# Half passes in the row halves of TensorE's array for the queries' projection, with other first stages, router products, last stages and order

## The reference

```python
# layer 0, attention: 32 heads, low rank (192) for queries, 64 for keys and values
q = rms_norm(x @ q_a_w, q_a_ln_w) @ q_b_w          # 192 = 128 + 64 rows of the product
ckv = x @ kv_a_w                                    # 64 latent, 64 rotary columns
scores = q_pass @ k_pass.T + rope(q_rot) @ rope(k_rot).T
out = softmax(causal(scores)) @ v @ o_w
# layer 0: graph attention on the context (top-k mask), then 7 experts, top 2, and a shared one
gate = x @ Wr + br                                  # 8 columns: the router
# layer 1: attention with 16 heads, bilinear attention on the context, feed-forward of 1024
h = silu(x @ w_gate.T) * (x @ w_up.T);  y = h @ w_down.T
```

## Time and profile before

| | |
|---|---|
| median of 3 runs | 673.74 us (673.16 to 674.34) |
| the profiled execution, its own time | 674.2 us |
| its span, first to last instruction | 672.3 us |
| PE busy | 651.7 us (97%), 5342 matmuls |
| DVE, ACT, POOL busy | 524.2, 502.5, 389.5 us |
| granted clock of TensorE | 0.997 |

### The profile page before, as it was taken

The page is one execution under the profiler, slowest core; times in us unless marked ns, Lnnn a source line. Parts: engine busy times, 40 slices in busy tenths (PEclk is TensorE's granted clock), DMA queues, the critical chain, the costliest instruction groups (busy, mean ns, idle before and its releaser), DMA issues.

```text
span 672.3 us, 15731 instructions
## 1 busy us (share of the span) xinstructions
PE 651.7 (97%) x5342; PEld 557.9 (83%) x5342; DVE 524.2 (78%) x1684; ACT 502.5 (75%) x1305; POOL 389.5 (58%) x646
## 2 busy tenths in 40 slices
PE   8899999999999999999999999999989999999996
PEld 5589988989888899889877888889878887778885
DVE  2799988996999799767889945557798878858455
ACT  4799778878688885898887866665658786876544
POOL 3388658457664845698769455545872321445543
PEclk9999999999999999999999999999999999999998
DMA  8763022214213211310032012111020000011201
GB/s 259 188 186 86 18 71 59 77 26 118 49 56 103 49 50 47 95 33 2 1 96 63 1 54 87 48 49 47 1 95 5 3 3 4 3 48 48 94 1 63
DMA packets 35048, 40.17 MB, mean 60 GB/s; under 512 B 7052, under 2 KB 27798, under 8 KB 34968
## 3 DMA queue, kind: packets, MB, share of 16 engines
q1 hardware_dynamic: 34424, 38.84, 19.8%
q10 hardware_dynamic: 544, 0.33, 0.2%
HBM read 29.05 MB, written 1.05 MB: 45 GB/s over the span
## 4 chain that ended last, share of the span: by engine, by line
PE 82%; DVE 7%; ACT 4%; SPq 2%; issue 2%; DMA 1%; POOL 1%; DVEq 0%; POOLq 0%; ACTq 0%
PE bank L1242 72%; PE bank L1256 8%; SPq L2762 1%; PE bank L1542 1%; ACT probs L1922 1%; DMA xT_plain<-in_xT 1%; POOL qT L2487 1%; DVE bn L2034 1%; DMA qT<-xT_plain 1%; DVE ctx_pair_lo L2011 1%; DVE y L2011 1%; DVE probs L2162 1%; DVE g_pair_lo L2011 0%; ACT x L1684 0%; ACT xT_hi L1677 0%
## 5 line engine op out<-in xcount | busy, mean ns | idle before, releaser
L2484 POOL TENSOR_SCALAR probs<-probs,soft 128x256 f32<-128x256 f32 (+1 forms) x256 | 104.9, 432 | 52.1 <-DVE soft L2170 51.0
L1784 ACT ACTIVATE probs<-probs,soft 128x256 f32<-128x256 f32 (+1 forms) x256 | 113.2, 448 | 12.0 <-DVE soft L2162 11.1
L2487 POOL TENSOR_TENSOR w_split_lo<-w_raw,w_split_hi 128x512 fp32r<-128x512 f32 (+2 forms) x57 | 74.3, 1311 | 67.9 <-ACT w_split_hi L1677 67.7
L1242 PE MATMUL bank<-xT_hi,w_split_hi 128*128 128x512 f32 x256 | 103.8, 405 | 3.7 <-DVE xT_lo L2014 2.5
L1242 PE MATMUL bank<-xT_lo,w_split_hi 128*128 128x512 f32 x256 | 100.5, 393 | 0.0
L1242 PE MATMUL bank<-keyT,qT 128*64 128x192 f32 (+3 forms) x1024 | 80.4, 302 | 1.3 <-POOL qT L2487 1.3
L1242 PEld LDWEIGHTS bank<-keyT,qT 128*64 128x64 f32 x1024 | 74.2, 137 | 8.9 <-issue 3.6
L1242 PE MATMUL bank<-xT_hi,w_split_lo 128*128 128x512 f32 x192 | 75.5, 393 | 0.0
L2487 POOL TENSOR_TENSOR qT<-qT,xT_plain 64x512 f32<-64x512 f32 x44 | 56.5, 1283 | 31.8 <-DMA qT<-xT_plain 29.7
L2162 DVE CUSTOM_DVE_ANT_0 probs<-bank,mask 128x128 f32<-128x128 f32 (+1 forms) x192 | 58.0, 330 | 17.2 <-PE bank L1242 16.2
L1677 ACT ACTIVATE probsT<-bank 128x384 f32<-128x384 f32 x128 | 53.6, 494 | 13.9 <-PE bank L1256 13.4
(11 more groups left out here) (259 smaller groups left out, 1820.6 us busy)
## 6 DMA issues: line engine op xcount, KB each, us to landing
qT<-xT_plain SPq DMA_DIRECT2D x88, 64.0 KB, 2.0
w_raw_heads<-in_w_o SPq DMA_DIRECT2D x8, 512.0 KB, 4.6
w_raw<-in_w_nopeT SPq DMA_DIRECT2D x8, 384.0 KB, 3.1
qT<-rope_buf SPq DMA_DIRECT2D x40, 64.0 KB, 2.0
w_raw<-in_w_gateT SPq DMA_DIRECT2D x8, 256.0 KB, 2.7
w_raw<-in_w_upT SPq DMA_DIRECT2D x8, 256.0 KB, 3.1
w_raw<-in_w_downT SPq DMA_DIRECT2D x8, 256.0 KB, 3.6
w_raw<-in_L_ffn_Wup SPq DMA_DIRECT2D x7, 256.0 KB, 2.6
```

Of the source, the lines that this page charges most:

```text
L1242: return t.matmul(out, lhsT, rhs, start=start, stop=stop, skip_group_check=shared)
L1784: ins = s.activation(p[:, at], p[:, at], ACT.Exp, bias=st[:, 0, r:r + 1], scale=-1.0, accum_out=st[:, 1, r:r + 1])
L2484: return g_.tensor_scalar(out, in0, s1, s2, op0, op1)
L2487: return g_.tensor_tensor(out, in0, in1, op)
```

## The change

1. `q` is cut in two steps. `q_full` makes the four whole-array matmuls of each bank. `q` makes the fifth of each bank over 64 rows alone: the rotary weights' hi rows now stand in rows 64 to 127 and the latent ones' in rows 0 to 63 (`rest_rows`), so the two matmuls lie in different row halves. The memset of `qaT.lo` goes.
2. The start: `down_T` loses the keys' transposes to a step `key_T`; DVE's `key_scale` is a step apart from `down_scale`; a Sqrt on ACT at the start loads its table early; the first q's wait for less (`TURNED_FOR`); `adj_w`, `adj_qk`, `adj_sim 0` and both `down` steps come earlier; the second load of tokens goes ahead of the first weights; the first `qT` buffer lies in other memory.
3. The router: the tokens are loaded and the router's weights, split in hi and lo (16 columns), stream; `route_gate` and ACT's copy go.
4. `out1` puts its two bias matmuls together.
5. The end: `f_end` is cut in `f_mid` (hidden tiles 4 to 6) and `f_end` (tile 7), in the order `f_mid 0, f_mid 2, f_end 0, f_mid 1, f_end 1`; the last store is issued by ACT.
6. PE's order and the due times are new throughout, and so are the planner's costs.

```diff
-down 0, w_k 0, down 1, w_q 0, down_T 0, w_v 1, w_k 1, q 0 0 0, down_T 1, w_q 1, adj_w, w_v 0, adj_qk, q 0 0 1,
-q 1 0 0, s 0 0 0, s 1 0 0, q 1 0 1, adj_sim 0, s 0 0 1, s 1 0 1, q 1 1 0, pT 0 0 0, q 1 1 1, pT 0 0 1, pT 1 0 0,
+down 0, down 1, w_k 0, adj_w, w_q 0, adj_qk, w_v 0, down_T 0, key_T 0, adj_sim 0, w_v 1, q_full 0 0 0, q 0 0 0,
+w_k 1, down_T 1, q_full 0 0 1, key_T 1, w_q 1, q 0 0 1, q_full 1 0 0, q 1 0 0, w_k 2, s 0 0 0, q_full 1 1 0, q 1 1 0,
...
+EVERY_TURNED = [(name, h) for h in range(NHALF) for name in ("down_T", "key_T")]
+TURNED_FOR = {("q", 0, 0, 0): [("down_T", 0)], ("q", 0, 0, 1): [("down_T", 0), ("key_T", 0)]}
+MID_TILES = [[(0, j) for j in range(TB)], *[[(1, j)] for j in range(TB)]]
+LAST_STORED = (B - 1, TB - 1)
...
+    def rest_rows(kind, low=False):
+        return slice(QREST, P) if (kind == 1) != low else slice(0, QREST)
...
                 for kind in (1, 0):
                     out = wait_bank(("q", n, g, p, ("lat", "rot")[kind]))[:, :]
                     first, rest = (w_q[:, c, kind, 2 * p:2 * p + 2, :] for c in range(2))
-                    mm3(out, first, qaT[:, 0, at], True, False)
-                    mm(out, rest.hi, qaT.hi[:, 1, at], False, False)
-                    mm(out, rest.hi, qaT.lo[:, 1, at], False, True).then_inc(q_ready.sem, 1)
+                    mm3(out, first, qaT[:, 0, at], True, False, True)
+                    mm(out, rest.hi, qaT.hi[:, 1, at], False, False, True)
+            elif name == "q":
+                n, g, p = k
+                rest, at = group_q(g).hi[:, 1, :, 2 * p:2 * p + 2, :], slice(n * HALF, (n + 1) * HALF)
+                for kind in (1, 0):
+                    rows = rest_rows(kind)
+                    mm(bank_of(("q", n, g, p, ("lat", "rot")[kind]))[:, :], rest[rows, kind, :, :], qaT.lo[rows, 1, at],
+                       False, True, True).then_inc(q_ready.sem, 1)
...
-                terms = [(c, plain(part)) for c in range(DC) for part in (xT_pair.hi, xT_pair.lo)]
-                for n, (c, xt) in enumerate(terms):
-                    for i, tile in enumerate(tiles_of[h]):
-                        ins = mm(out[32 * i:32 * i + NE, 0:P], w_router[:, c, :], xt[:, c, tile * P:(tile + 1) * P],
-                                 n == 0, n == len(terms) - 1, True)
+                terms = [(part, c) for c in range(DC) for part in (xT_pair.hi, xT_pair.lo)]
+                for i, tile in enumerate(tiles_of[h]):
+                    for n, (part, c) in enumerate(terms):
+                        ins = mm(out[:, i * 2 * NE:(i + 1) * 2 * NE], part[:, c, tile * P:(tile + 1) * P],
+                                 w_router_parts[:, c, :, :], i == 0 and n == 0, n == len(terms) - 1, True)
...
                 for i in range(TB):
+                    mm(out[:, i * D:(i + 1) * D], ones1[:, :], bias1[:, 3 * D:], i == 0, False, True)
+                for i in range(TB):
                     part = out[:, i * D:(i + 1) * D]
-                    mm(part, ones1[:, :], bias1[:, 3 * D:], i == 0, False, True)
...
-f_up 1 7, f_end 0, f_end 1""")
+f_up 1 3, f_down 0 7, f_down 1 1, f_up 1 5, f_down 1 2, f_up 1 6, f_down 1 3, f_up 1 7, f_mid 0, f_mid 2, f_end 0,
+f_mid 1, f_end 1""")
...
+                    w.wait_ge(*zeroed["unit"])
+                    s.activation(last_root[:, 0:1], plain(ones1[:, 0:1]), ACT.Sqrt)
...
+        b, i = LAST_STORED
+        w.wait_ge(*last_normed[b, i])
+        s.dma_start(out_dram[b, i * P:(i + 1) * P, :], x[:, TB * b + i, :]).then_inc(stored[b], 16)
```

More of the change, by code:

```diff
@@ L431, in make_plan @@
         if n < U_EXPERT:
-            stage(("load", n, 0), "SP 2.6, DMA 2.5, WAY 2", *needs)
+            stage(("load", n, 0), "SP 2.6, DMA 2.5, WAY 2", *needs,
+                  *[By(("load", first), "SP") for first, then in LOADS_AFTER if n == then])
             stage(("load", n, 1), "SP 1.15, DMA 2.0, WAY 2", *[("w_v", n - 2)] if n >= 2 else [])
@@ L449, in make_plan @@
-        stage(("down_T", h), "PE 1.4, ACT 1.65, DVE 1.35", ("down_scale", h), ("down_rope", h), ("load", "identity"),
-              holds=[bank("qaT", h, c, left=(("down_T", h), "DVE")) for c in range(2)]
-              + [bank("keyT", h, left=(("down_T", h), "ACT"))], items=3)
-        stage(("key_swap", h), "SP 1.2, DMA 0.8, WAY 2", By(("down_T", h), "ACT"))
+        stage(("down_scale", h), "POOL 1.25, ACT 1.4", ("down_root", h), ("load", "const"), items=4)
+        stage(("key_scale", h), "DVE 0.95", ("down_root", h), ("load", "const"))
@@ L454, in make_plan @@
+        stage(("down_T", h), "PE 0.9, ACT 1.1, DVE 1.35", ("down_scale", h), ("load", "identity"),
+              holds=[bank("qaT", h, c, left=(("down_T", h), "DVE")) for c in range(2)], items=2)
+        stage(("key_T", h), "PE 0.45, ACT 0.55", ("key_scale", h), ("down_rope", h), ("load", "identity"),
+              holds=[bank("keyT", h, left=(("key_T", h), "ACT"))])
+        stage(("key_swap", h), "SP 1.2, DMA 0.8, WAY 2", By(("key_T", h), "ACT"))
     for g in range(NG):
         before = [] if g < 2 else [s for part in unit_readers(g - 2) for s in part]
-        stage(("w_k", g), "PE:cols64 0.7, ACT 0.85", ("load", g, 0),
+        stage(("w_k", g), "PE:cols64 0.65, ACT 0.65", ("load", g, 0),
@@ L493, in make_plan @@
     for b in range(B):
-        stage(("adj_sim", b), "PE:rows64 0.95, ACT:exp 1.5", ("adj_qk",),
+        stage(("adj_sim", b), "PE:rows64 1.02, ACT:exp 1.5", ("adj_qk",),
               *[("adj_mask", b - 1, i) for i in range(TB) if b],
@@ L512, in transposed @@
         step = ("xT", tag, b)
-        stage(step, "PE 0.42, ACT 0.5" + ("" if tag == "bilinear" else ", DVE 0.62"), *needs, ("load", "identity"),
+        stage(step, "PE 0.455, ACT 0.5" + ("" if tag == "bilinear" else ", DVE 0.62"), *needs, ("load", "identity"),
               holds=[bank(*step, left=(step, last))])
@@ L538, in make_plan @@
         for h in range(NHALF):
-            stage(("e_u", e, h), "PE 2.79, ACT 2.5, DVE 1.3", ("split", U_EXPERT + e, 0), *[("xT", "experts", b) for b in halves(h)],
+            stage(("e_u", e, h), "PE 2.79, ACT 2.5, DVE 1.5", ("split", U_EXPERT + e, 0), *[("xT", "experts", b) for b in halves(h)],
                   *MOE_ROOM_LEFT, holds=[bank("e_u", e, h, i, left=(("e_u", e, h), "ACT")) for i in range(DC)]
```

271 lines of the change are left out of this document (142 added, 129 removed), and 7 rows, old and new, of the table ASIDE.

## The result

The changed kernel is slower: 678.41 us (median of five, 677.93 to 679.85) against 673.76 us for the kernel before on the same chip (673.16 to 675.02). The ratio is 1.0067, 95% interval 1.0050 to 1.0083: 4.65 us more, where 1.5 us less was forecast. The profiled execution took 679.64 us, 677.8 of them span.

A forecast was written before the change was run, and what follows sets the result against it. PE was taken as the bound, busy 651.7 of 672.3 us. Terms +0.1 + 3.3 - 3.3 - 0.4 - 0.3 - 1.2 + 0.4 = -1.4, rounded to -1.5, gave 672.2 us; 8-in-10 range 668.0 to 676.5.

The forecast's parts named there:

- The half passes: In the `q` steps: 7.3 us gross gain against 7.4 us for 37 changes of array division, net +0.1 us.
- a lone one costs 0.63 and replaces 0.46: A single half pass between whole steps takes 0.23 + 0.40 = 0.63 us where the replaced matmuls took 0.46.
- the one price of 0.20: Each of the 37 changes of array division belonging to half passes was priced at 0.20 us, 7.4 us in all.
- The order's other changes of division: 22 more changes of array division from the new PE order, at 0.15 us each: +3.3 us (bounds 2.3 and 5.1).
- The start: Up to the first `q`: some 4.6 us of waiting and hidden time could go, 3.3 taken as gained: -3.3 us.
- The second tokens are issued ahead of the weights: At the start: part of why the first half's root comes earlier, within the -3.3 us; no size of its own.
- it fills what is left of the wait: PE work moved ahead of `q_full 0 0 0` fills the remaining wait before the first `q`; within the -3.3 us.
- The second rival: Start gives nothing, first `q_full` waiting for `qaT.lo` until 24.4 us or later: 675.5 us; chance 0.22.
- The third rival: Rotary chain late because `q_ready` comes only with the half pass; three more waits for `qT`, +3, 675.2 us; chance 0.10.
- The router: Both halves together 2.7 us before, 2.4 after at 0.075 per 16-column matmul; with four fewer division changes -0.4 us.
- The middle and out1: Last expert to first `s1`: reordered steps cover waits, -1.2 us; `out1` loses a restart in four calls, -0.3 us.
- The end: Batch 2 ready 0.7 us later with DVE the bound, last store on ACT saves 0.3: +0.4 us.

The follow-up runs named there:

- run 2: Kernel before with the half passes alone, at the end of each `q` step, nothing else moved: 676.24 us, before 674.43.
- run 1: Changed kernel with each of the 32 half passes turned back into two whole-array matmuls: 680.12 us, before 674.48.
- Run 7: Kernel before with SP issuing the third weights' load ahead of the swaps of the first q and the keys: 675.83 us, before 674.43.
- run 9: Changed kernel with the ten small router and bias loads moved on SP behind the swaps of `q 0 1 0`: 679.66 us, before 674.60.
- run 8: Changed kernel, SP's router and bias loads behind the first three q's swaps: 682.38 us; with `adj_sim 0` also later on ACT: 685.89; before 675.44.
- run 11: Kernel before with the changed middle and `out1` alone: 675.68 us; with the changed end alone: 675.43 us; before 674.66.
- run 10: Changed kernel with router loads late on SP, router matmuls widened to 128 columns, `out 3 6` ahead of `out 3 7`: 677.98 us, before 674.60.
- runs 6: Changed kernel, `adj_sim 0` (ACT) and third weights' load (SP) later: 687.92 us, before 674.43; with `w_k 2` also later: 685.57, before 674.66.

## Why the prediction was wrong, by its own steps

- **The half passes (+0.1 us): mechanism right, 0.9 too dear.** The pair, its start 0.32 behind a whole one and the way back were as priced. Measured -0.8 to -0.9. The step "a lone one costs 0.63 and replaces 0.46" is right within 0.02 ahead of a whole step (run 2). Too dear was the one price of 0.20 for every change: beside steps in row halves, and where two half passes stand in a row, less is lost (run 1).
- **The order's other changes of division (+3.3): about right.** PE's steps from 0 to the router, without waits, take 0.55 us more, and `down_T` with `key_T` 1.4 less (2.75 against 4.15 for `down_T` before). That leaves 1.95 for this term and the half passes, so some 2.8 for this term. It was not isolated further.
- **The start (-3.3, bounds 0 to -4.6): the step that failed.** I took 3.3 of 4.6 us as gained; the trace has +1.4 at the first point of equal work and +1.6 at the end of the attention. Two parts of it were wrong. "The second tokens are issued ahead of the weights" brought them 0.35 earlier, but the third load of tokens landed 2.3 later, and the order has `down 1`, which reads it, right behind `down 0`: PE waits for it until 12.84, and `w_q 0` starts at 19.02 (16.75 before). The first matmul of `down 0` is later too: 6.5 to 7.9 in all twelve profiled executions of kernels built on the changed one, against 6.0 to 6.5 in the eight built on the kernel before. No run moved these loads back, so how much of the 1.4 they bring is argued from the traces alone. And "it fills what is left of the wait" holds for the first `q_full`, but I did not ask what is late next: the work that fills it puts a load in front of the first q's swaps on SP. The second rival had the direction right (675.5, measured 678.4), and its point of decision (first `q_full` at 22.8 or later) was passed at 25.13, but not for its reason, `qaT.lo`. The third rival's mechanism came true beside it, with two waits of 2.2 and 0.9, by SP's queue and not by the place of the half passes. Run 7 shows that SP's order makes such a wait. Taking it away gave 0.5 us by the router in run 9, and in run 8, where the same loads then held `probs`, the router began 3.7 later.
- **The router (-0.4, bounds -0.8 to +0.8): mis-sized, and it lacked a term.** I took 0.075 us for a matmul of 16 columns and ruled out more than the unhidden load's 0.11. It is 0.106 to 0.111, so the two products cost 3.5 us against 2.2 for both halves before: +1.3 of PE's work. The term had 2.7 for both halves before, with the wait of 0.39 counted in; so taken it is +0.9, just outside its bounds. Since waits hide part of it, the changed kernel's stretch to the last `e_down` is 0.5 longer with the widened product than with the old one (149.8 against 149.3, both at full clock). The Trainium skill, TensorE: Matmul & The Clock Gate (LDWEIGHTS), gives P / 1.2 ns for a load of P columns whatever the number of rows, so by an estimate from it 107 ns for these 128; the trace agrees with 0.109 on average. The fall of the clock, 1.5 us in an execution where it happens, was not thought of. It is in the profiled execution and is not what makes the median: the changed kernel's three executions at a mean clock of 0.998 took 677.93 to 678.41 us, the two at 0.995 took 679.64 and 679.85.
- **Waits in the attention and the experts: not foreseen.** `out 3 5` (1.04), `out 3 7` (0.92) and `e_down 0 1` (1.53, `g_pair_lo`) stand too close behind what they read.
- **The middle and out1 (-1.5): right in place,** -1.3 from `e_down 3 0` to the first `f_up`. In the kernel before the same edit gave its gain back, mostly by a fall of the clock (run 11).
- **The end (+0.4): right,** +0.57, and 0.54 alone.

Without the fall of the clock, the table's parts sum to 4.0 us: start and attention +2.8, router and experts +1.4, middle -1.3, FFN and end +1.1. The medians differ by 4.65. What stays open: 0.5 us between the first `f_up` and `f_up 1 7`, and in run 10 some 1.3 us between the start and the router that no recorded wait explains; half of that the changed kernel has as well, as work of PE (0.66 from the first point of equal work to the router).

## What to carry to other kernels

A step that fills a wait brings its loads, copies and table loads along; follow those through each in-order queue and ask what is late next, above all what the issuing queue now has in front of the next critical transfer. In a tightly ordered kernel single repairs moved the wait (3.8, 2.6, 3.3 us in runs 6 and 8) more often than they removed it, so a gain at one point is to be read again at the next point of equal work. A split into array halves is to be priced by its neighbours: it paid only beside steps that divide the array anyway, and in twos. And a new wait of PE can cost more than its length: in runs 6 and 8 waits of 0.6 and 1.4 us stood ahead of seven at the lower clock, so the windows' clock is to be read before time is put down to a wait.

## What the runs showed of the hardware that was not expected

- Two half passes in a row share what a change costs. The second pair starts 0.34 us behind the first; its weight loads start 0.11 behind the first pair, in five of the six places, so they overlap with it. The next whole step begins 0.32 behind the second pair, where it begins 0.43 behind a lone one. Two in a row take 0.05 to 0.11 us less than the four whole matmuls in their place (run 1), a lone one between whole steps 0.17 more (run 2).
- A matmul of 16 columns with new 128 x 128 weights takes as long as one of 128 columns, 0.11 us. Behind sixteen of the narrow ones the clock fell to 1.2 GHz in six of nine executions although PE was never idle for more than 0.3 us in that stretch, and in none of ten behind wide or old ones.
- The clock also fell at places that differ between kernels, mostly behind waits of PE: at 24 to 29, 34 to 43, 45 to 49, 59 to 65 and 494 to 515 us, for 3 to 7 us each. That is likely part of why single executions of one kernel spread over 4 us and more (kernel before: 672.1 to 679.2 in 29 runs). Of its 97 executions in the five groups of the experiments, the 26 with a mean clock of 0.998 and more have a median of 673.5 us and the 43 with 0.996 and less 675.2; it was not tested by a run.
